# Moving the background matmuls of a fused attention and feed-forward kernel by one step

## The chip, the core and the metric
The kernel runs on one core of a Trainium2 chip. The metric is device time in microseconds: the median of three runs of the kernel before is 1022.14 us (1021.96 to 1023.54). The profiled execution is one of them and took 1021.96 us; its span, from the first to the last instruction, is 1020.1 us.

## The reference
One transformer layer with the norm after each part, in float32. There are 2 batches of 1024 rows of 512 columns.

```python
Q = (x @ Wq.T + bq)            # 32 query heads of 16
K = (x @ Wk.T + bk); V = (x @ Wv.T + bv)   # 8 key/value heads of 16
Q, K = _rope(Q, K)
scores = einsum('bhqd,bhkd->bhqk', Q, repeat(K, 4)) / sqrt(16)
w = softmax(scores)
attn = einsum('bhqk,bhkd->bhqd', w, repeat(V, 4))
x = layernorm(x + attn @ Wo.T + bo)
hdn = silu((x @ gate_w.T) * gate_s) * ((x @ up_w.T) * up_s)   # 1408 wide
x = layernorm(x + (hdn @ down_w.T) * down_s)
```

## The kernel before, in words
The five engines run programs of their own (`tensor`, `scalar`, `vector`, `gpsimd`, `sync` in the code, PE, ACT, DVE, POOL and SP in the profile), in order, and wait for each other through semaphores. A number in float32 is often held as a rounded high part and a low part, so that a product takes three fast matmuls (high by high, high by low, low by high).

Attention runs in 256 steps, numbered u, written (n, v) with u = 16n + v. There are 16 groups n (batch by key/value head). Eight steps are one pass over the 1024 keys for 512 queries, so "step 3 of 8" below means u % 8 == 3. In each step PE does, for g in 0 to 3, one score matmul of head g (`scores`, L478), which goes into one of three score banks in turn, and half of a maximum step (`advance`, `maxima_half`, L456), which computes scores that are only needed for their row maxima, some twelve steps ahead. Once per step it does `weigh` (L497), the product of the previous step's exponentials with V: after g = 3 in an even step, after g = 2 in an odd one. ACT takes the exponentials (L797); DVE takes the maxima, per step one whole reduction over two banks (L1008, 128x1024) and one in two halves (L1004, 128x512 each), the halves so that PE can refill a bank sooner. Two pairs of banks take the maximum steps in turn. The row maxima of sixteen maximum steps are complete at the end of each step 3 of 8: DVE joins them (L1024), POOL splits them in two parts (L1326), DVE transposes them (L1041), and in step 4 of 8 SP writes them to DRAM (`write_max`, L1572), waits until that has landed, and reads them back beside Q (L1575). The scores of the pass that begins four steps later wait for this (`max_in`, L471), since the maxima are subtracted inside the score matmul.

Eleven larger pieces of matmul work lie between the steps: six projections of Q or K for later heads (`project_at`, 24 matmuls each, L400), one product for V of batch 1 (`values_at`, 32 matmuls of 128x128, L437) and four parts of the output projection of batch 0 (`out_at`, 24 matmuls each, L523). `background(u)` issues one on PE. It needs two of the three score banks: `free_banks(u)` takes the bank just written by a score, and the one after it in turn. ACT (`evacuate_raw`, L783) or DVE (`add_values` L987, `add_rows` L1077) empties them. `norm_at` puts a layer norm of the rows of the piece before on DVE (`first_norm`, L1053 to L1061), which waits once for POOL. After a projection SP swaps halves by DMA (`swap_halves`), POOL rotates (`rope`), and ACT and POOL split the result (`rope_end`).

SP issues nearly all DMAs, on one queue and in program order: `gather` (L1557, L1563) brings K and Q of group n + 2 in twelve DMAs, `recip_at` sends reciprocals of the softmax sums out (L1602) and back broadcast (L1608), `finish` writes a pass's result (L1585). The eleven weight blocks of the feed-forward part are loaded (768 KB each, L1519, `A<-in_wf`) at the steps in `ffn_at`; at the steps in `low_at` POOL adds up their low bits (`add_low`, L1405 and L1407), which gives the flag by which the feed-forward part takes its path. That part follows from about 733 us on and is bound by PE.

Of the kernel before, what the change touches and what calls it, by code (L numbers as in the profile page):

```python
# [70 lines left out]
def post_ln_layer(nc, xT_d, x_d, wqk_d, wv_d, bqk_d, bv_d, wo_d, bo_d, wf_d, gs_d, us_d, ds_d,  # L71
# [6 lines left out]
    with ExitStack() as ctx:  # L78
# [121 lines left out]
        def bank(i):  # L200
            return PS2[:, i, :] if i < 3 else PV[:, :]
# [57 lines left out]
        stream = [(n, qt, g) for n in range(NG) for qh in range(2) for qt in range(4 * qh, 4 * qh + 4)  # L259
                  for g in (2, 0, 3, 1)]  # L260
        jobs = [(0, 1), (0, 2), (0, 3), (1, 4), (1, 0), (1, 1), (1, 2), (1, 3)]
        project_at = {(1, 10): 2, (4, 10): 3, (5, 2): 4, (6, 2): 5, (8, 2): 6, (8, 10): 7}
        rope_end = {(0, 1): (0, "h0"), (0, 2): (0, "h1"), (0, 3): (0, "out"),
                    (0, 4): (1, "rope"), (0, 8): (1, "h0"), (0, 10): (1, "h1"), (0, 11): (1, "out")}
        for at_u, j in project_at.items():
            u0 = 16 * at_u[0] + at_u[1] + 8
            rope_end.update({divmod(u0, 16): (j, "h0"), divmod(u0 + 2, 16): (j, "h1"), divmod(u0 + 3, 16): (j, "out")})
        values_at = (2, 10)
        out_at = {(10, 2): 0, (10, 10): 1, (11, 2): 2, (11, 10): 3}
        norm_at = {(10, 10): 0, (11, 2): 1, (11, 10): 2}  # L270
        recip_at = {(2, 13): 0, (4, 13): 1, (6, 5): 2, (8, 5): 3, (10, 5): 4, (12, 5): 5, (14, 5): 6}
        divide_at = {divmod(16 * n + v + 6, 16): kc for (n, v), kc in recip_at.items()}
        gather_at = {(n, {0: 13}.get(n, 5)): n + 2 for n in range(NG - 2)}
        x_at = {(part // 2, 8 * (part % 2)): (0, part) for part in range(4)}
        x_at.update({(2 + part // 2, 5 + 8 * (part % 2)): (1, part) for part in range(4)})
        ffn_at, low_at = {}, {}
        for i in range(FI):
            ffn_at.setdefault(divmod((181, 184, 189, 192, 204, 205, 207, 209, 221, 223, 228)[i], 16), []).append(i)
            low_at.setdefault(divmod(180 + 8 * (1, 1, 2, 3, 4, 4, 5, 5, 6, 6, 7)[i], 16), []).append(i)
        before_flag = 508  # L280

        crosswise = (0, 2, 1, 3)
# [37 lines left out]
        score_bank = {}  # L320
# [13 lines left out]
            return c if p == len(pieces(c)) - 1 else (c, p)  # L334

        def free_banks(u):
            last = score_bank[4 * u + 1, 0]
            return (last + 1) % 3, last

        def ffn_slots(x):  # L340
# [34 lines left out]
        def tensor(e):  # L375
# [335 lines left out]
            for u in range(SPLIT):  # L711
                at_u = divmod(u, 16)
                for g in range(4):
                    scores(u, g)
                    advance(1)
                    if len(pieces(4 * u + g)) == 2:
                        scores(u, g, 1)
                    if g == 1:
                        background(u)
                    if u >= 1 and g == (3, 2)[u % 2]:  # L720
                        weigh(u - 1)
                if at_u == (15, 1):
                    flag_sum()
                if at_u == (15, 2):
                    w.wait_ge(*dve_flag.at("flag"))
# [12 lines left out]
        def scalar(e):  # L738
# [190 lines left out]
            for u in range(SPLIT):  # L929
                at_u = divmod(u, 16)  # L930
                for g in range(4):
                    exponent(u, g)
                    if g == 1 and at_u in project_at:
                        for h, i in enumerate(free_banks(u)):
                            evacuate_raw(project_at[at_u], h, i)
                if u >= 1:
                    finish(u - 1)
                if at_u in rope_end and rope_end[at_u][1] in ("h0", "h1"):
                    round_half(rope_end[at_u][0], int(rope_end[at_u][1] == "h1"))
                if at_u == (15, 2):  # L940
                    w.wait_ge(*dve_flag.at("flag"))
# [11 lines left out]
        def vector(e):  # L953
# [318 lines left out]
            for u in range(SPLIT):  # L1272
                at_u = divmod(u, 16)
                maximum(next(steps))
                k = next(steps)
                if at_u in norm_at:
                    first_norm(False, 0, norm_at[at_u])
                if at_u == values_at:
                    for h, i in enumerate(free_banks(u)):
                        add_values(1, h, i)  # L1280
                if at_u in out_at:
                    add_rows(False, 0, out_at[at_u], [bank(i) for i in free_banks(u)])
                maximum(k)
                if at_u in recip_at:
                    reciprocal(recip_at[at_u])
                if at_u == (15, 0):
                    w.wait_ge(*pool_low.at((FI - 1, 2)))
                    e.tensor_reduce(lowb[:, :], lowsum, AX.X, ALU.max).then_inc(*dve_flag.next("max"))
                if at_u == (15, 1):
                    w.wait_ge(*pe_flag.at())  # L1290
                    e.tensor_scalar(flag[0:1, 0:1], slot_pair(before_flag % 2)[0:1, 0, 0:1], 0.0, None,
                                    ALU.is_gt).then_inc(*dve_flag.next("flag"))
                if at_u == (15, 2):
                    w.wait_ge(*dve_flag.at("flag"))
# [11 lines left out]
        def gpsimd(e):  # L1306
# [161 lines left out]
            for u in range(SPLIT):  # L1468
# [2 lines left out]
                    spread_of(2, (False, 0, norm_at[at_u]))  # L1471
                if u % 8 == 3 and apart(steps_done(u) // 16 - 1):
                    split_max(steps_done(u) // 16 - 1)
                if u >= 1 and divmod(u - 1, 16) in project_at:
                    rope(project_at[divmod(u - 1, 16)])
                if at_u in divide_at:
                    divide(divide_at[at_u])
                if at_u in rope_end:
# [367 lines left out]
```

## Time and profile before

| what | value |
|---|---|
| median of three runs | 1022.14 us |
| profiled execution | 1021.96 us |
| its span | 1020.1 us |
| PE busy | 1006.1 us (99%) |
| DVE busy | 797.0 us (78%) |
| ACT busy | 665.5 us (65%) |
| POOL busy | 274.2 us (27%) |
| chain that ended last | PE 93%, DVE 2% |
| mean granted clock of PE | 0.997 |

Busy time of PE counts overlapping matmuls and modelled ends, so 99% does not say that PE had no time to spare. What limits a stage is read from the gaps of the other engines in that stage, below.

### The profile page before, as it was taken

How to read it: one execution, taken by the hardware profiler on the slowest of the kernel's cores; microseconds unless marked ns; L12 is line 12 of the kernel's file. 1: busy time of each engine (PE TensorE's matmuls, PEld its weight loads, DVE VectorE, ACT ScalarE, POOL GpSimd, SP SyncE). 2: the span in 40 equal slices, each digit the busy share in tenths (PEclk: the TensorE clock that was granted, in tenths of full speed). 3: DMA queues.
4: the chain of work that ended last, by engine and by line, in shares of the span. 5: the costliest groups of instructions: out<-in, count | busy, mean ns of one | idle time of the engine just before them, and what ended most of it. 6: DMA issues, size and time to landing. Idle time of an engine off the chain costs nothing.

```text
span 1020.1 us, 15669 instructions
## 1 busy us (share of the span) xinstructions
PE 1006.1 (99%) x5852; PEld 532.3 (52%) x5852; DVE 797.0 (78%) x1131; ACT 665.5 (65%) x1345; POOL 274.2 (27%) x284
## 2 busy tenths in 40 slices
PE   8999999999999999999999999999999999999996
PEld 4643435334444333443444433333358888888885
DVE  6999797999787999779899999999713666562635
ACT  5179796888787988779767688888862430222221
POOL 4461030251245541246301063456000001000002
PEclk9999999999999999999999999999999999999998
DMA  6175316233224522444150447422438112221011
GB/s 245 50 208 137 94 55 203 59 97 92 55 81 116 101 81 42 83 104 111 35 81 13 121 140 167 105 100 63 150 109 221 63 42 58 67 65 19 0 42 44
DMA packets 64289, 94.81 MB, mean 93 GB/s; under 512 B 37520, under 2 KB 37776, under 8 KB 62128
## 3 DMA queue, kind: packets, MB, share of 16 engines
q1 hardware_dynamic: 63776, 93.10, 34.3%
q8 instruction: 48, 0.79, 0.3%
q10 hardware_dynamic: 432, 0.66, 0.2%
q14 instruction: 33, 0.27, 0.1%
HBM read 53.88 MB, written 27.00 MB: 79 GB/s over the span
## 4 chain that ended last, share of the span: by engine, by line
PE 93%; DVE 2%; issue 2%; POOL 1%; DMA 1%; ACT 0%; SPq 0%; POOLq 0%; DVEq 0%
PE PS L478 29%; PE PV L497 25%; PE PSA L567 16%; PE PS L584 6%; PE PSA L456 5%; PE PS L400 4%; PE PS L523 2%; PE PSA L523 2%; PE PV L584 2%; PE PS L437 1%; DMA A<-in_cosT 1%; DVE A L965 0%; ACT Bn L797 0%; PE PV L437 0%; PE PS L567 0%
## 5 line engine op out<-in xcount | busy, mean ns | idle before, releaser
L797 ACT ACTIVATE Bn<-PS 128x512 f32<-128x512 f32 x1128 | 536.2, 558 | 87.6 <-PE PS L478 74.5
L456 PE MATMUL PSA<-Kt,Qt 48*128 48x512 f32 x1010 | 382.9, 459 | 0.5 <-DVE nmx L1008 0.4
L478 PE MATMUL PS<-Qt,Kt 50*128 50x512 f32 x1128 | 382.0, 434 | 1.3 <-ACT Bn L797 1.1
L478 PEld LDWEIGHTS PS<-Qt,Kt 50*128 50x128 f32 x1128 | 183.3, 184 | 304.4 <-ACT Bn L797 279.0
L1004 DVE TENSOR_REDUCE nmx<-PSA 128x1 f32<-128x512 f32 x488 | 310.7, 677 | 30.8 <-PE PSA L456 30.8
L1008 DVE TENSOR_REDUCE nmx<-PSA 128x1 f32<-128x1024 f32 x261 | 317.4, 1218 | 19.5 <-PE PSA L456 16.5
L497 PE MATMUL PV<-Bn 128*32 128x512 f32 x2048 | 272.8, 605 | 0.0
L456 PEld LDWEIGHTS PSA<-Kt,Qt 48*128 48x128 f32 x1010 | 173.0, 183 | 8.6 <-issue 2.2
L567 PE MATMUL PSA<-x1Th,wr 128*128 128x512 f32 x344 | 135.3, 393 | 0.0
L567 PE MATMUL PSA<-x1Tl,wr 128*128 128x512 f32 x344 | 134.3, 390 | 0.0
L833 ACT ACTIVATE sg<-PSA,gs 128x512 f32<-128x512 f32 x43 | 29.7, 690 | 128.1 <-PE PSA L567 128.1
L1109 DVE SCALAR_TENSOR_TENSOR sg<-PSA,us,sg 128x512 f32<-128x512 f32 x43 | 32.2, 749 | 91.5 <-ACT sg L833 91.5
L1326 POOL CAST msp<-nmx 128x16 fp32r<-128x16 f32 x30 | 5.9, 198 | 285.0 <-DVE nmx L1024 285.0
L497 PEld LDWEIGHTS PV<-Bn 128*32 128x32 f32 x2048 | 40.3, 108 | 76.0 <-issue 65.0
L567 PEld LDWEIGHTS PSA<-x1Th,wr 128*128 128x128 f32 x344 | 64.6, 188 | 17.9 <-issue 3.6
L567 PEld LDWEIGHTS PSA<-x1Tl,wr 128*128 128x128 f32 x344 | 64.6, 188 | 13.4
L1412 POOL TENSOR_SCALAR ve<-mv 128x2 f32<-128x2 f32 (+1 forms) x11 | 2.9, 260 | 252.7 <-DVE mv L1056 252.7
L1129 DVE TENSOR_TENSOR hTl<-sg,hTh 128x512 fp32r<-128x512 f32 x38 | 27.9, 734 | 33.1 <-ACT hTh L846 33.0
L846 ACT CAST hTh<-sg 128x512 fp32r<-128x512 f32 x38 | 23.6, 621 | 43.9 <-DVE sg L1109 36.8
L584 PE MATMUL PS<-wr,hTh 128*128 128x512 f32 x114 | 44.6, 391 | 0.0
L584 PE MATMUL PS<-wr,hTl 128*128 128x512 f32 x114 | 44.5, 390 | 0.0
L1407 POOL TENSOR_TENSOR lowsum<-lowsum,lowf 128x512 f32<-128x512 f32 x32 | 41.0, 1282 | 2.6
(174 smaller groups left out, 896.0 us busy)
## 6 DMA issues: line engine op xcount, KB each, us to landing
Qt<-pscr SPq DMA_DIRECT2D x90, 128.0 KB, 5.2
A<-in_wf SPq DMA_DIRECT2D x11, 768.0 KB, 5.5
wr<-A SPq DMA_DIRECT2D x33, 256.0 KB, 2.8
pscr<-A SPq DMA_DIRECT2D x16, 512.0 KB, 3.5
vscr<-Bn SPq DMA_DIRECT2D x32, 256.0 KB, 2.7
Kt<-pscr SPq DMA_DIRECT2D x90, 64.0 KB, 2.7
A<-A SPq DMA_DIRECT2D x16, 256.0 KB, 3.7
Bn<-vscr SPq DMA_DIRECT2D x8, 512.0 KB
```

Of the source, the lines that this page charges most:

```text
L400: op = e.matmul(ps, v, t, start=first and i == 0, stop=last and end)
L456: op = e.matmul(slot_pair(s)[:, h, :], Qt[n % 3][p:p + NC_, g % 2, 128 * qt:128 * qt + 128], Kt[n % 3][p:p + NC_, 512 * h:512 * h + 512], ...
L478: e.matmul(score_tile(i)[:, cols], Kt[n % 3][rows, 128 * kt:128 * kt + 128], Qt[n % 3][rows, g % 2, 512 * qh + cols.start:512 * qh + cols. ...
L497: op = e.matmul(PV[32 * g:32 * g + 32, :], Bn[:, o:o + 32], Pb[c % NP_], start=(kt == 0), stop=(kt == 7), tile_position=(0, 32 * g))
L523: op = e.matmul(ps, t_, v, start=(k == 0 and i == 0), stop=(k == KT - 1 and i == len(pairs) - 1))
L567: op = e.matmul(gate_bank(x, q, j), v, t, start=(k == 0 and m == 0), stop=(k == KT - 1 and m == (1 if x else 0)))
L584: op = e.matmul(bank(t), v, t_, start=(i == 0 and m == 0), stop=(i == FI - 1 and end))
L797: e.activation(Pb[c % NP_][:, cols], score_tile(score_bank[c, p])[:, cols], ACT.Exp, scale=0.25).then_inc(*act_exp.next(piece(c, p)))
L1004: e.tensor_reduce(col, slot_pair(s)[:, h, :], AX.X, ALU.max, negate=True).then_inc(*dve_max[s].next((k, 0) if h == 0 else k))
L1008: e.tensor_reduce(nmx[:, hh % 2, c0:c0 + 1], slot_pair(s), AX.XY, ALU.max, negate=True).then_inc(*dve_max[s].next(k))
L1109: e.scalar_tensor_tensor(out=out, in0=gate_bank(x, q, 1), scalar=us[:, i:i + 1], in1=sg[q % 2], op0=ALU.mult, op1=ALU.mult).then_inc(*dve_ ...
L1407: e.tensor_tensor(lowsum, lowsum, lowf, ALU.add).then_inc(*pool_low.next((i, j)))
```

## The change
The eleven background pieces move from steps 2 of 8 to steps 3 of 8, and inside the step from behind g = 1 to behind g = 2 (all eleven steps are now odd), directly ahead of `weigh`. `free_banks` and ACT's evacuation follow. On DVE, in the steps of the values and of the output projection, the split maximum is taken apart: its first half stands ahead of the norm and the additions, its second half behind them. The second parts of `rope` stay in the steps where they were, `divide` comes two steps earlier, and the tables of weight loads and of POOL's sums are replaced by a formula.

```diff
-        project_at = {(1, 10): 2, (4, 10): 3, (5, 2): 4, (6, 2): 5, (8, 2): 6, (8, 10): 7}
+        project_at = {(1, 11): 2, (4, 11): 3, (5, 3): 4, (6, 3): 5, (8, 3): 6, (8, 11): 7}
-            u0 = 16 * at_u[0] + at_u[1] + 8
+            u0 = 16 * at_u[0] + at_u[1] + 7
-        values_at = (2, 10)
-        out_at = {(10, 2): 0, (10, 10): 1, (11, 2): 2, (11, 10): 3}
-        norm_at = {(10, 10): 0, (11, 2): 1, (11, 10): 2}
+        values_at = (2, 11)
+        out_at = {(10, 3): 0, (10, 11): 1, (11, 3): 2, (11, 11): 3}
+        norm_at = {(10, 11): 0, (11, 3): 1, (11, 11): 2}
-        divide_at = {divmod(16 * n + v + 6, 16): kc for (n, v), kc in recip_at.items()}
+        divide_at = {divmod(16 * n + v + 4, 16): kc for (n, v), kc in recip_at.items()}
-            ffn_at.setdefault(divmod((181, 184, 189, 192, 204, 205, 207, 209, 221, 223, 228)[i], 16), []).append(i)
-            low_at.setdefault(divmod(180 + 8 * (1, 1, 2, 3, 4, 4, 5, 5, 6, 6, 7)[i], 16), []).append(i)
+            ffn_at.setdefault(divmod(11 * 16 + 5 + 8 * (i // 2) + 3 * (i % 2), 16), []).append(i)
+            low_at.setdefault(divmod(11 * 16 + 4 + 8 * (1, 1, 2, 3, 3, 4, 4, 5, 5, 6, 7)[i], 16), []).append(i)
...
-            last = score_bank[4 * u + 1, 0]
+            last = score_bank[4 * u + 2, 0]
...
-                    if g == 1:
+                    if u >= 1 and g == (3, 2)[u % 2]:
                         background(u)
-                    if u >= 1 and g == (3, 2)[u % 2]:
                         weigh(u - 1)
...
-                    if g == 1 and at_u in project_at:
+                    if g == 2 and at_u in project_at:
...
-                if at_u in norm_at:
-                    first_norm(False, 0, norm_at[at_u])
-                if at_u == values_at:
...
-                maximum(k)
+                if at_u in norm_at or at_u in out_at or at_u == values_at:
+                    maximum(k, (0,))
+                    if at_u in norm_at:
+                        first_norm(False, 0, norm_at[at_u])
...
+                    maximum(k, (1,))
+                else:
+                    maximum(k)
...
-                if u >= 1 and divmod(u - 1, 16) in project_at:
-                    rope(project_at[divmod(u - 1, 16)])
+                if at_u in project_at:
+                    rope(project_at[at_u])
```

The loads stood at steps 181, 184, 189, 192, 204, 205, 207, 209, 221, 223 and 228; they stand at 181, 184, 189, 192, 197, 200, 205, 208, 213, 216 and 221 now.

On PE, around the product for V (L437), step (2, 10) of the kernel before. L478 is a score, L456 a maximum half, L497 `weigh`:

```order
L478 MATMUL PS<-Qt_109,Kt_110 128x512
L456 MATMUL PSA<-Kt_106,Qt_105 128x512
L437 MATMUL PS<-A 128x128 x32
L478 MATMUL PS<-Qt_109,Kt_110 128x512
L456 MATMUL PSA<-Kt_106,Qt_105 128x512
L478 MATMUL PS<-Qt_109,Kt_110 128x512
L456 MATMUL PSA<-Kt_106,Qt_105 128x512
L497 MATMUL PV<-Bn 32x512 x4
```

The same place in the changed kernel, step (2, 11):

```order
L478 MATMUL PS<-Qt_109,Kt_110 128x512
L456 MATMUL PSA<-Kt_106,Qt_105 128x512
L437 MATMUL PS<-A 128x128 x32
L497 MATMUL PV<-Bn 32x512 x4
L478 MATMUL PS<-Qt_109,Kt_110 128x128
L456 MATMUL PSA<-Kt_106,Qt_105 128x512
```

Two maximum halves stood between the piece and `weigh`; now `weigh` follows directly, and the maximum half behind it is the second of a split one.

On DVE, around the norm and additions of step (10, 10) of the kernel before. L1008 is a whole maximum, L1004 a half, L1053 to L1061 the norm, L1077 the additions, L1024 the join:

```order
L1008 TENSOR_REDUCE nmx<-PSA 128x1
L1053 BN_STATS st<-x1a 128x6 x2
L1056 BN_AGGR mv<-st 128x2 x2
L1061 TENSOR_SCALAR x1a<-x1a,mv,ve 128x512 x2
L1077 TENSOR_TENSOR x1a<-x1a,PS 128x512 x2
L1004 TENSOR_REDUCE nmx<-PSA 128x1 x2
L1008 TENSOR_REDUCE nmx<-PSA 128x1
L1004 TENSOR_REDUCE nmx<-PSA 128x1 x2
L1024 TENSOR_TENSOR nmx<-nmx 128x8
```

The same in the changed kernel, step (10, 11), where every line number is one lower:

```order
L1007 TENSOR_REDUCE nmx<-PSA 128x1
L1003 TENSOR_REDUCE nmx<-PSA 128x1
L1052 BN_STATS st<-x1a 128x6 x2
L1055 BN_AGGR mv<-st 128x2 x2
L1060 TENSOR_SCALAR x1a<-x1a,mv,ve 128x512 x2
L1076 TENSOR_TENSOR x1a<-x1a,PS 128x512 x2
L1003 TENSOR_REDUCE nmx<-PSA 128x1
L1023 TENSOR_TENSOR nmx<-nmx 128x8
```

The vector work lies between the two halves of one maximum, and the join comes directly after the second half.

On SP, steps 197 to 209 of the kernel before. `Kt` and `Qt<-pscr` are a gather, `vscr` a pass's result, `mscr` the maxima on their way out and in, `in_wf` the weight blocks:

```order
L1563 DMA Qt_109<-pscr 16x2048 x6
L1585 DMA vscr<-Bn 128x512
L1572 DMA mscr<-mrow 4x32x32
L1575 DMA Qt_107<-mscr 2x2x512 x2
L1519 DMA A<-in_wf 128x1536 x3
L1585 DMA vscr<-Bn 128x512
L1519 DMA A<-in_wf 128x1536
```

The same in the changed kernel:

```order
L1566 DMA Qt_109<-pscr 16x2048 x6
L1522 DMA A<-in_wf 128x1536
L1588 DMA vscr<-Bn 128x512
L1522 DMA A<-in_wf 128x1536
L1575 DMA mscr<-mrow 4x32x32
L1578 DMA Qt_107<-mscr 2x2x512 x2
L1522 DMA A<-in_wf 128x1536
L1588 DMA vscr<-Bn 128x512
L1522 DMA A<-in_wf 128x1536
```

Two weight blocks that stood behind the maxima's way out and in now stand ahead of it.

## Rows read from the trace of the kernel before

**Rows 1.** DVE's timeline, steps without a piece; start, duration, line, count, [idle before <-releaser].

```profile
301.00 1.22 DVE L1008 TENSOR_REDUCE nmx<-PSA 128x1 f32<-128x1024 f32 x1 [0.16 <-PE PSA L456]
...
305.94 1.23 DVE L1008 TENSOR_REDUCE nmx<-PSA 128x1 f32<-128x1024 f32 x1 [0.17 <-PE PSA L456]
...
307.08 1.28 DVE L1004 TENSOR_REDUCE nmx<-PSA 128x1 f32<-128x512 f32 x2
...
308.55 1.22 DVE L1008 TENSOR_REDUCE nmx<-PSA 128x1 f32<-128x1024 f32 x1
```

**Rows 2.** DVE's timeline around the projection of step (1, 10).

```profile
119.29 1.23 DVE L1008 TENSOR_REDUCE nmx<-PSA 128x1 f32<-128x1024 f32 x1 [0.16 <-PE PSA L456]
...
127.88 1.29 DVE L1004 TENSOR_REDUCE nmx<-PSA 128x1 f32<-128x512 f32 x2 [5.02 <-PE PSA L456]
129.77 1.22 DVE L1008 TENSOR_REDUCE nmx<-PSA 128x1 f32<-128x1024 f32 x1 [0.60 <-PE PSA L456]
...
132.38 1.22 DVE L1008 TENSOR_REDUCE nmx<-PSA 128x1 f32<-128x1024 f32 x1
```

**Rows 3.** PE's timeline around the same projection.

```profile
121.52 0.50 PE L400 MATMUL PS<-xh,wh 128*128 128x512 f32 x1
...
127.31 0.50 PE L478 MATMUL PS<-Qt,Kt 50*128 50x512 f32 x1
...
127.97 1.07 PE L497 MATMUL PV<-Bn 128*32 128x512 f32 x8
128.97 0.50 PE L478 MATMUL PS<-Qt,Kt 50*128 50x512 f32 x1
```

**Rows 4.** DVE's timeline, output projection with norm, step (10, 10).

```profile
521.26 1.22 DVE L1008 TENSOR_REDUCE nmx<-PSA 128x1 f32<-128x1024 f32 x1
...
534.31 1.22 DVE L1008 TENSOR_REDUCE nmx<-PSA 128x1 f32<-128x1024 f32 x1
```

**Rows 5.** Timeline of DVE and PE around the product for V, step (2, 10).

```profile
164.33 1.23 DVE L1008 TENSOR_REDUCE nmx<-PSA 128x1 f32<-128x1024 f32 x1 [0.17 <-PE PSA L456]
...
166.66 7.38 PE L437 MATMUL PS<-A 128*128 128x128 f32 x64
...
179.03 1.22 DVE L1008 TENSOR_REDUCE nmx<-PSA 128x1 f32<-128x1024 f32 x1
```

**Rows 6.** Timeline of ACT, exponentials ahead of step (1, 10) and in an undisturbed step 3.

```profile
120.98 0.49 ACT L797 ACTIVATE Bn<-PS 128x384 f32<-128x384 f32 x1
...
305.67 0.60 ACT L797 ACTIVATE Bn<-PS 128x512 f32<-128x512 f32 x1
```

**Rows 7.** Timeline of POOL and DVE around the projection of step (6, 2).

```profile
322.48 1.27 POOL L1352 TENSOR_TENSOR wl<-A,wh 128x512 fp32r<-128x512 f32 x1
...
330.10 1.29 DVE L1004 TENSOR_REDUCE nmx<-PSA 128x1 f32<-128x512 f32 x2 [5.77 <-PE PSA L456]
```

**Rows 8.** SP's timeline, from the end of a gather in step 197 on.

```profile
617.68 0.42 SPq L1585 DMA_DIRECT2D vscr<-Bn  x1
625.63 0.56 SPq L1572 DMA_DIRECT2D mscr<-mrow  x1
630.25 0.54 SPq L1575 DMA_DIRECT2D Qt<-mscr  x2
...
645.33 0.56 SPq L1572 DMA_DIRECT2D mscr<-mrow  x1
647.30 0.55 SPq L1575 DMA_DIRECT2D Qt<-mscr  x2
```

**Rows 9.** Busy time by stretch; the last two columns are DMA share and GB/s.

```profile
612.00:624.00 12.00, 12.00 (x83) 4.47 (x79) 11.76 (x15) 10.88 (x25) 0.24 (x1) 1.00 0.87 134
...
632.00:640.00 8.00, 8.00 (x56) 3.02 (x52) 7.85 (x11) 7.68 (x18) 1.24 (x1) 1.00 0.99 393
```

**Rows 10.** Timeline of PE and DVE where step 208 begins.

```profile
632.99 0.40 PE L456 MATMUL PSA<-Kt,Qt 48*128 48x512 f32 x1
...
633.86 1.22 DVE L1008 TENSOR_REDUCE nmx<-PSA 128x1 f32<-128x1024 f32 x1
```

More of the change, by code:

```diff
@@ L1275, in vector @@
                 k = next(steps)
-                if at_u in norm_at:
-                    first_norm(False, 0, norm_at[at_u])
-                if at_u == values_at:
[L1279 to L1282, printed above, removed]
-                maximum(k)
+                if at_u in norm_at or at_u in out_at or at_u == values_at:
+                    maximum(k, (0,))
+                    if at_u in norm_at:
+                        first_norm(False, 0, norm_at[at_u])
+                    if at_u == values_at:
+                        for h, i in enumerate(free_banks(u)):
+                            add_values(1, h, i)
+                    if at_u in out_at:
+                        add_rows(False, 0, out_at[at_u], [bank(i) for i in free_banks(u)])
+                    maximum(k, (1,))
+                else:
+                    maximum(k)
                 if at_u in recip_at:
```

## The prediction
> **What bounds the kernel now.** I read the page's engine shares first (they are in the table above): PE is busy 99% of the span, DVE 78%. Since that share counts modelled and overlapping matmuls, it does not tell who sets the pace of attention, so I took DVE's timeline in steps without a background piece [rows 1]. From the whole maximum at 301.00 to the same one two steps later, at 305.94, it is 4.94 us, and the only gap is 0.17 us. DVE's maxima set the pace, at 2.47 us a step; PE and ACT have slack there. So time is lost where DVE stands idle, and the reader is to look at DVE's gaps rather than at PE's work.
>
> Such gaps stand at each of the eleven background pieces. At step (1, 10) DVE waits 5.02 us for PE and then, once more, 0.60 us [rows 2]: PE is on the projection from 121.52 to 127.31, 5.79 us, issues two maximum halves and then does `weigh` from 127.97 to 128.97, 1.00 us [rows 3]. To price a piece I measure from the whole maximum of step 1 of 8 to the first one behind the join, in step 4 of 8. Without a piece that is 308.55 - 301.00 = 7.55 us [rows 1]. With the projection it is 132.38 - 119.29 = 13.09 [rows 2], with an output part 534.31 - 521.26 = 13.05 [rows 4], with the product for V 179.03 - 164.33 = 14.70 [rows 5]. A piece costs 5.54, 5.50 and 7.15 us now.
>
> **The change, part 1: the new place of the pieces.** The PE work is the same, so only the waits differ. I build the changed stretch by putting the projection into the quiet step of rows 1.
> - Start. A piece needs the bank behind the last score's, which in an odd step is that of g = 0, so it waits for that exponential. It runs from 305.67 for 0.60, to 306.27 [rows 6]. The piece starts 0.05 later, as it does before (120.98 + 0.49 = 121.47 [rows 6], start 121.52 [rows 3]): 306.32.
> - It takes 5.79: 312.11. `weigh` follows at once and takes 1.00: 313.11. Only then comes the maximum half. From PE's start of a score and half to DVE's start it is 127.88 - 127.31 = 0.57 [rows 2, 3]: DVE starts at 313.68.
> - The half takes 0.64 (half of the 1.28 for two [rows 1]): 314.32. From there to the next whole maximum, over the join, it is 308.55 - 308.36 = 0.19 [rows 1]: 314.51.
> - Without the piece this maximum starts at 308.55. The piece costs 5.96 us, against 5.54: plus 0.42.
>
> The 0.60 gap behind the piece does go, since the next maximum half is ready when the first is done; but `weigh` now lies inside the first gap and lengthens it by its 1.00. DVE's supply at the piece's start is nearly the same: here to 307.08 + 0.64 = 307.72, 1.40 us; before it ended at 127.88 - 5.02 = 122.86, 1.34 us [rows 1 to 3].
>
> For six projections this is 6 x 0.42 = 2.5 us. For the four output parts the way is the same (the norm and the first addition lie inside PE's piece in both orders, the second addition under `weigh` now), the new cost 5.96 less at most 0.1 for a slightly shorter piece: 5.9 - 5.5 = 0.4 each, 1.6 us. For V the piece takes 7.38 instead of 5.79 [rows 5]: 5.96 + 1.59 - 7.15 = 0.4. Together 4.5 us. What is not in the rows is how ACT and PE refill the banks right behind the piece; I bound a piece's difference by -0.58 (the 1.00 of `weigh` wholly hidden) and +0.7, and take 0.42, which follows the rows.
>
> One piece was late for another reason. At (6, 2) POOL ends the split of the weights only at 322.48 + 1.27 = 323.75, and DVE's gap is 5.77 instead of 5.02 [rows 7]. The piece is now needed one step, 2.47 us, later, behind 323.75: minus 0.75.
>
> Part 1: 4.5 - 0.75 = plus 3.7 us, from -7 to +7 by the bounds (11 x -0.58 - 0.75 and 11 x 0.7 - 0.75).
>
> **Part 2: the weight loads.** Two blocks of 768 KB move from steps 204 and 205 to 197 and 200. SP comes to them at about 617.7, right behind a gather [rows 8]. There the DMA engines are full: share 0.87 at 134 GB/s from 612 to 624 [rows 9]. Even without them the maxima's write of step 204 lands late: from its issue to the read's it takes 630.25 - 625.63 = 4.62 us, against 647.30 - 645.33 = 1.97 in a calm place [rows 8]. So something was still queued in front of it until about 630. Now 1.57 MB more is. At 393 GB/s, the rate of such loads [rows 9], that is 4.0 us at most of the engines' time; three blocks shared that stretch with a copy, and engines that were idle towards the end take a little of it. I take 3.7: the write has landed at 630.25 + 3.7 = 633.95.
>
> The read of the maxima must have landed before the scores of step 208. Before, PE started them at 632.99 without a gap [rows 10], at most 2.74 us behind the read's issue. With a read that takes between 1.97, as the write did, and 2.74, step 208 begins at 635.9 to 636.7, 2.9 to 3.7 us late. DVE has no supply but the split maximum in hand, and its next one starts at 633.86 without a gap [rows 10], so the delay passes to it whole. I take 3.2 us. The bounds are 0 (small transfers find free engines, or the backlog in front of them was not the same engines') and 4.2.
>
> The Trainium skill, in "DMA: Bandwidth & Descriptors", section "Queues, rings and completion order", says that each DMA engine takes its descriptors in the order of its ring, and that the semaphore fills only when every engine involved is through. The 4.62 us of rows 8 agree. By this rule the write cannot pass the loads, and the full term of part 2 stands; if small transfers passed large ones, the sum would lack 3.2 us.
>
> The later blocks (205, 208, 213, 216, 221) lie ahead of writes with more room and replace loads that were there. The blocks on POOL's list move with them; POOL is busy 27% of the span (same table).
>
> **Part 3: what costs nothing.** `divide` two steps earlier runs while POOL is idle, ahead of the next split of maxima. `rope` stays in its step; its data come later, since the swap's DMA now starts about when the join is due, and ACT asks for the rotated half only seven steps, 7 x 2.47 = 17 us, later. The swap's DMA also comes closer ahead of the maxima's write of the next step. If it cost nothing there, the read would have its usual room: the write is issued about four steps, 9.9 us, less the 1.4 us from the join, before the scores that need it, and takes 1.97, the read up to 2.74; that leaves over 3 us as cover, and if that were gone each microsecond over it would be lost at six places.
>
> **Sum.** 1021.96 (the profiled execution) + 3.7 + 3.2 = 1028.9 us. The median before is 0.2 us above that execution, so it stands for either; I say 1028.7.
>
> **Rivals.**
> - Only part 1. The maxima's write gets through, or the read is quick: 1025.7. For it: the delay needs the same engines to be backlogged; against it: the 4.62 us.
> - Only part 2. The new place costs nothing, because the two gaps merely change places: 1021.96 + 3.2 - 0.75 = 1024.4.
> - Neither: 1021.2 to 1022.5. For it: DVE's idle time per piece is mostly PE's 5.8 us in either order.
> - Faster. The gap behind `weigh` (0.60) goes and nothing takes its place, because PE enters the piece at 306.02 rather than 306.32 and DVE's work under it reaches to the end of `weigh`. Eleven pieces at -0.58 and the 0.75: 1021.96 - 7.1 = 1014.9. It decides at the first maximum half behind the piece: this rival needs DVE to start it not later than 6.4 us after PE enters the piece, as before (121.52 to 127.88). That the half stands behind `weigh` in the order speaks against it.
> - Slower still. The swap's DMA ahead of each of six maxima writes takes away more than the 3 us of cover, so that the scores of the next pass wait about 1 us at each: 1028.7 + 6 = 1035. Against it: the sizes above.
>
> **How the numbers follow.** Both parts 0.45; only part 1 0.22; only part 2 0.06; neither 0.10; faster 0.10; slower still 0.07. A difference under 0.2%, 2 us, can't be told from none here. Slower than 1024.2 are the first case, most of the second and of the third, and the last: 0.75. Same: 0.10 and 0.05 of the second and third: 0.15. Faster: 0.10. The range of 8 in 10 goes from 1022.5 to 1031.5: it leaves out the faster case, the slowest one and a few in a hundred of "neither". The likeliest case's own range is 1026 to 1031.
>
> **What the profile after would show.** At each projection one DVE gap of about 5.9 to 6.0 us before a single half (L1003), and no 0.60 gap behind it; from the whole maximum of step 1 to the one behind the join 13.5 us instead of 13.09. The gap at (6, 3) is like the others. On SP, two weight loads directly behind the gather, the maxima's write of step 204 landing 8 us or more after its issue, and the scores of step 208 waiting some 3 us for a DMA. I am wrong on part 1 if that distance stays 13.1 or falls; on part 2 if PE has no gap where step 208 begins; and on part 3 if scores wait at other passes, or ACT waits for POOL in the splits behind a projection.

## The result and the profile after

The changed kernel takes 1032.09 us (median of 4 runs, 1030.91 to 1033.06), the kernel before 1022.84 in the same comparison: a ratio of 1.0094, with a 95% interval of 1.0083 to 1.0106. Predicted were 1028.7 us and a range of 1022.5 to 1031.5. The direction and both places were right; the sum was 3.4 us short. The profiled execution of the changed kernel took 1032.56 us, its span is 1030.7 (1020.1 before).

I place the difference by DVE's joins. The join (L1024 before, L1023 after) comes once in 8 steps, so its distances cut attention into equal pieces. Worked out from the starts of these rows on DVE's timeline, in us:

| interval that holds | before | after | difference |
|---|---|---|---|
| nothing, behind quiet steps | 19.70 to 19.83 | the same | 0 |
| projection (1, 10) / (1, 11) | 25.27 | 25.76 | +0.49 |
| product for V | 26.91 | 27.35 | +0.44 |
| projections 3, 4 | 25.21, 25.33 | 25.70, 25.83 | +0.49, +0.50 |
| projection (6, 2) / (6, 3) | 26.05 | 25.64 | -0.41 |
| projections 6, 7 | 25.17, 25.25 | 25.62, 25.74 | +0.45, +0.49 |
| output parts, four | 25.24, 25.33, 25.21, 25.19 | 25.71, 25.80, 25.76, 25.76 | +0.47, +0.47, +0.55, +0.57 |
| the start of step 208 | 19.70 | 25.29 | +5.6 |

The pieces' rows add up to +4.5. The quiet intervals right behind a piece are longer by 0.03 to 0.13, and all quiet intervals up to step 208 together by +0.7. From there to the end the two kernels run alike. So part 1 cost 5.2 us (forecast 3.7) and part 2 5.6 us (forecast 3.2).

DVE's timeline of the changed kernel around the projection of (1, 11) (start, duration, line, count, idle before and releaser) answers to [rows 2]:

```profile
119.08 1.23 DVE L1007 TENSOR_REDUCE nmx<-PSA 128x1 f32<-128x1024 f32 x1 [0.17 <-PE PSA L456]
...
131.75 0.69 DVE L1003 TENSOR_REDUCE nmx<-PSA 128x1 f32<-128x512 f32 x1 [5.89 <-PE PSA L456]
132.54 0.17 DVE L1023 TENSOR_TENSOR nmx<-nmx 128x8 f32<-128x8 f32 x1
132.62 1.22 DVE L1007 TENSOR_REDUCE nmx<-PSA 128x1 f32<-128x1024 f32 x1
```

There is one gap of 5.89 us ahead of a single half and none of 0.60 behind it. From whole maximum to whole maximum it is 132.62 - 119.08 = 13.54 us (forecast 13.5, before 13.09 [rows 2]). PE's timeline at the projection of (8, 3) shows the order inside the gap: the bank's wait, the piece, `weigh` (L497) and then the next maximum half. It answers to [rows 3]:

```profile
412.27 0.39 PE L478 MATMUL PS<-Qt,Kt 50*128 50x512 f32 x1
...
413.12 0.50 PE L400 MATMUL PS<-xh,wh 128*128 128x512 f32 x1 [0.22 <-ACT Bn L796]
...
418.79 1.07 PE L497 MATMUL PV<-Bn 128*32 128x512 f32 x8
419.79 0.32 PE L478 MATMUL PS<-Qt,Kt 50*128 50x128 f32 x1
```

SP's timeline of the changed kernel answers to [rows 8]. Two weight loads (L1522) are issued where there were none, and the maxima's write of step 204 (L1575) is followed by its read (L1578) 8.04 us later, not 4.62:

```profile
622.46 0.42 SPq L1522 DMA_DIRECT2D A<-in_wf  x1
622.93 0.43 SPq L1588 DMA_DIRECT2D vscr<-Bn  x1
623.40 0.43 SPq L1522 DMA_DIRECT2D A<-in_wf  x1
630.60 0.56 SPq L1575 DMA_DIRECT2D mscr<-mrow  x1
638.64 0.56 SPq L1578 DMA_DIRECT2D Qt<-mscr  x2
```

PE's timeline at the start of step 208 answers to [rows 10]:

```profile
637.77 0.39 PE L478 MATMUL PS<-Qt,Kt 50*128 50x384 f32 x1
640.71 0.46 PE L478 MATMUL PS<-Qt,Kt 50*128 50x512 f32 x1 [2.55 <-DMA Qt<-mscr]
...
641.86 0.79 PE L456 MATMUL PSA<-Kt,Qt 48*128 48x512 f32 x1
642.58 1.93 PE L497 MATMUL PV<-Bn 128*32 128x512 f32 x8
```

and DVE's timeline there:

```profile
641.48 1.22 DVE L1007 TENSOR_REDUCE nmx<-PSA 128x1 f32<-128x1024 f32 x1 [2.55 <-PE PSA L456]
642.62 1.28 DVE L1003 TENSOR_REDUCE nmx<-PSA 128x1 f32<-128x512 f32 x2
645.74 1.22 DVE L1007 TENSOR_REDUCE nmx<-PSA 128x1 f32<-128x1024 f32 x1 [1.84 <-PE PSA L456]
...
648.60 0.69 DVE L1003 TENSOR_REDUCE nmx<-PSA 128x1 f32<-128x512 f32 x1 [1.04 <-PE PSA L456]
```

The wait that was forecast is 2.55 us. But two more gaps follow, 1.84 and 1.04, that no DMA ends. A matmul takes 0.79 us where it took 0.50 [rows 3], `weigh` 1.93 instead of 1.07. The busy time by stretch (engines' busy time, then the granted clock, the DMA share and GB/s) shows what goes with them; it answers to [rows 9]:

```profile
612.00:624.00 12.00, 12.00 (x83) 4.60 (x75) 11.94 (x16) 10.90 (x25) 4.92 (x5) 1.00 0.57 97
630.00:636.00 6.00, 6.00 (x43) 2.17 (x37) 6.00 (x10) 5.01 (x11) 4.63 (x6) 1.00 0.98 262
636.00:640.00 4.00, 2.16 (x17) 0.65 (x15) 2.81 (x4) 2.29 (x5) 3.64 (x5) 1.00 0.18 66
...
642.00:648.00 6.00, 6.00 (x26) 1.49 (x26) 3.72 (x5) 3.44 (x7) 1.18 (x1) 0.50 0.47 140
648.00:650.00 2.00, 2.00 (x11) 1.03 (x11) 1.39 (x2) 1.60 (x4) 0.00 (x0) 0.93 0.64 258
```

Behind the wait the granted clock of TensorE is 0.50, its lower level of 1.2 GHz, for some 7 us. The sum of the three gaps, 5.43 us, is nearly the +5.6 of the table. The prediction had no term for the clock.

### The profile page after: what moved, and what is told of

The parts are those of the page before. It is cut to its first block, busy times and chain, and to the rows that moved or that the text cites. A ratio compares the mean times of both kernels' runs of the same rounds, so it can differ in the third digit from the quotient of the medians.

```text
span 1030.7 us, 15669 instructions
## 1 busy us (share of the span) xinstructions
PE 1012.3 (98%) x5852; PEld 531.0 (52%) x5852; DVE 798.3 (77%) x1131; ACT 665.6 (65%) x1345; POOL 274.4 (27%) x284
## 4 chain that ended last, share of the span: by engine, by line
PE 91%; DVE 3%; issue 2%; DMA 2%; POOL 1%; ACT 1%; SPq 0%; POOLq 0%; DVEq 0%
PE PS L478 29%; PE PV L497 24%; PE PSA L567 15%; PE PS L584 6%; PE PSA L456 5%; PE PS L400 4%; PE PS L523 2%; PE PSA L523 2%; PE PV L584 2%; ACT Bn L796 1%; DMA mscr<-mrow 1%; PE PS L437 1%; DMA A<-in_cosT 1%; DVE nmx L1007 1%; DVE nmx L1003 0%
## 5 line engine op out<-in xcount | busy, mean ns | idle before, releaser
L478 PE MATMUL PS<-Qt,Kt 50*128 50x512 f32 x1128 | 386.0, 436 | 4.0 <-DMA Qt<-mscr 2.5
L456 PE MATMUL PSA<-Kt,Qt 48*128 48x512 f32 x1010 | 386.2, 460 | 0.5 <-DVE nmx L1007 0.4
L478 PEld LDWEIGHTS PS<-Qt,Kt 50*128 50x128 f32 x1128 | 183.1, 185 | 312.2 <-ACT Bn L796 285.0
L497 PE MATMUL PV<-Bn 128*32 128x512 f32 x2048 | 274.5, 608 | 0.0
L456 PEld LDWEIGHTS PSA<-Kt,Qt 48*128 48x128 f32 x1010 | 174.4, 184 | 9.1 <-issue 2.2
L497 PEld LDWEIGHTS PV<-Bn 128*32 128x32 f32 x2048 | 40.4, 108 | 76.3 <-issue 65.6
L1394 POOL TENSOR_TENSOR Bn<-Bn 128x1024 f32<-128x1024 f32 x8 | 19.1, 2383 | 98.9 <-DMA Bn<-rscr 98.9
```

Of the source, the lines that this page charges most:

```text
L456: op = e.matmul(slot_pair(s)[:, h, :], Qt[n % 3][p:p + NC_, g % 2, 128 * qt:128 * qt + 128], Kt[n % 3][p:p + NC_, 512 * h:512 * h + 512], ...
L478: e.matmul(score_tile(i)[:, cols], Kt[n % 3][rows, 128 * kt:128 * kt + 128], Qt[n % 3][rows, g % 2, 512 * qh + cols.start:512 * qh + cols. ...
L497: op = e.matmul(PV[32 * g:32 * g + 32, :], Bn[:, o:o + 32], Pb[c % NP_], start=(kt == 0), stop=(kt == 7), tile_position=(0, 32 * g))
```

## The experiments

The theory: part 1 costs about 5 us because a piece and `weigh` now lie in one stretch of PE without a score between them; part 2 costs a wait of 2.5 us behind two weight loads and some 3 us of half clock that the wait sets off. The rivals are in the expectations. All ratios are to the kernel before in the same comparison.

**The two parts apart.** e1 is the changed kernel with the old tables for the loads and for POOL's sums, e2 the kernel before with the new ones. Of e1's edit, the line for the loads:

```diff
-            ffn_at.setdefault(divmod(11 * 16 + 5 + 8 * (i // 2) + 3 * (i % 2), 16), []).append(i)
+            ffn_at.setdefault(divmod((181, 184, 189, 192, 204, 205, 207, 209, 221, 223, 228)[i], 16), []).append(i)
```

> The changed kernel with the tables of weight loads and of POOL's sums of the kernel before; the pieces stay at steps 3 of 8. Theory (the moved pieces cost about 5 us by themselves; the two loads at steps 197 and 200 make the maxima's write of step 204 late by 3.4 us, PE then idles 2.5 us and its clock falls to half for some 7 us, 5.6 us in all): the wait at step 208 and the half clock are gone, the write lands about 4.6 us after its issue, the time is 5 to 6 us under the changed kernel's, some 5 us (0.5%) over the kernel before. Rival (the loss at step 208 comes from the new place of the pieces or from the earlier divide, which move the whole schedule of DMAs): the wait and the loss of 5.6 us stay, time as the changed kernel, 0.9% over before.

> The kernel before with the new tables of weight loads and of POOL's sums alone; the pieces stay at steps 2 of 8. Theory: the wait at step 208 appears with the half clock behind it, plus 5 to 6 us over the kernel before (0.5 to 0.6%); the join distances at the eleven pieces stay at 25.2 us. Rival (the loads matter only together with the moved pieces): no wait at step 208, time as before.

e1: 1027.16 us, ratio 1.0046 (1.0033 to 1.0059), the intervals with pieces as in the changed kernel, 19.75 us at step 208. e2: 1028.10 us, ratio 1.0059 (1.0046 to 1.0072), intervals with pieces as before, and at step 208 24.17 instead of 19.70. With before at 1022.32 there, the parts are 4.8 and 5.8 us by the medians. They add up to 10.6, as much as the spans of the two kernels differ (the medians differ by 9.3), and neither is nothing. In e2's trace part 2 is smaller, 24.17 - 19.70 = 4.5 us, because the clock is low for some 3 us there and not for 7, although its wait is longer (2.81). Another 1.2 us of e2's profiled execution stand ahead of the join at 88.51 (87.30 before), where the clock falls too; see the last section. On SP's timeline of e1 write and read stand 3.01 us apart, less than the 4.62 of the kernel before, which no run explains:

```profile
630.78 0.56 SPq L1575 DMA_DIRECT2D mscr<-mrow  x1
633.79 0.54 SPq L1578 DMA_DIRECT2D Qt<-mscr  x2
```

and on that of e2 8.21 us:

```profile
627.07 0.56 SPq L1572 DMA_DIRECT2D mscr<-mrow  x1
635.28 0.56 SPq L1575 DMA_DIRECT2D Qt<-mscr  x2
```

e2 shows the clock's fall without the moved pieces. In its stretches the clock (third column from the end) is 0.50 with DMA share 0.00:

```profile
636.00:638.00 2.00, 0.60 (x6) 0.54 (x6) 0.00 (x0) 0.09 (x1) 1.86 (x3) 1.00 0.58 122
638.00:640.00 2.00, 1.81 (x14) 0.38 (x10) 1.82 (x3) 1.97 (x4) 1.86 (x3) 0.75 0.67 280
640.00:642.00 2.00, 2.00 (x14) 0.83 (x6) 0.60 (x1) 0.91 (x2) 0.82 (x1) 0.50 0.00 0
```

**One load instead of two.** e4 is the changed kernel with block 5 back at step 205; block 6 goes from 205 to 207, behind the write and the read in either place.

> The changed kernel with one of the two loads, block 5, put back from step 200 to step 205; block 4 stays at 197. Theory (each 768 KB ahead of the maxima's write costs its share of 3.4 us, and PE's room at step 208 is under 1 us): the write lands about 6.3 us after its issue instead of 8.0, PE idles about 0.8 us at step 208, the clock stays up, and the time is 4 to 5 us under the changed kernel's (0.5% over before). Rival (the wait is there as soon as any load stands ahead): the write lands 8 us after its issue and the time is as the changed kernel's.

Write and read stand 6.03 us apart (633.84 to 639.87), PE's gap is 0.54 us, and the interval takes 20.38 us, 0.6 over the quiet one; the clock stays up there. The forecast for the write was 6.3. So the second 768 KB cost 2.0 us (8.04 - 6.03), the first 1.4 to 3.0 (against 4.62 before and 3.01 in e1), and nearly all of part 2 hangs on the second load, since only with it the wait gets long. The time, 1030.07 us (ratio 1.0063, 1.0047 to 1.0078), is 2.0 us under the changed kernel's and not the 4 to 5 that were expected. It scatters from 1027.3 to 1032.06. The profiled execution (1030.87, mean clock 0.996) has a fall of the clock at 63 to 68 us; the two fastest, 1027.3 and 1027.91, have mean clocks of 0.997 and 0.999. The interval, 4.9 us under the changed kernel's 25.29, says more than the median.

**The wait filled.** Into PE's wait at step 208 go 13 matmuls of 48 rows (e3), five fp32 ones of 128 rows (e7) or three such (e11). The expectations of e7 and e11 also name POOL's split of e6, below, but their kernels do not have it: the interval of (6, 3) is 25.64 in both, as in the changed kernel, and the 0.9 us that they count for it could not come. The edit of e11:

```diff
+                if at_u == (13, 0):
+                    clear(bank_free[score_bank[4 * u, 0]])
+                    for _ in range(3):
+                        e.matmul(score_tile(score_bank[4 * u, 0]), Vflat[:, 0:128], Vflat[:, 0:512], start=True, stop=True)
```

> The changed kernel with 13 matmuls of 48 rows by 512 columns more on PE where step 208 begins, into the score bank that the next score overwrites: 13 x 0.23 = 3.0 us of work whose result nobody reads. Theory (3.1 of the 5.6 us are the half clock, and the clock falls because PE idles 2.5 us): the granted clock stays at its upper level (2.4 GHz) around step 208, DVE's gaps of 1.84 and 1.04 us behind the first one vanish, the first one grows by 0.3 to 0.5 us, and the time is 2.5 to 3 us under the changed kernel's (0.65% over before). Rival (the clock falls for another reason, for instance the DMA traffic, or the gaps of 1.84 and 1.04 us are not the clock's): the time grows by up to 0.5 us, the later gaps stay.

> The changed kernel with five fp32 matmuls of 128 rows by 512 columns put into TensorE's wait at step 208 (into a bank that is free by then), and POOL's split for (6,3) ahead of the bias addition. The same place filled with 48-row score matmuls did not hold the clock. Theory: with the array fully used through the wait the granted clock stays at 1.00 behind it, and the interval there goes from 25.3 to about 22.5 us (the 2.5 us wait itself stays, the some 3 us at half clock go); with -0.9 at (6,3) the time is about 1028.5. Rival A: the clock falls to 0.50 behind the wait whatever TensorE does in it (its cause is elsewhere, in the bulk loads or in the stretch before), 25.3 us stays, 1031. Rival B: the five matmuls run at fp32's four passes and last longer than the wait: 26 us or more, 1032.

> The changed kernel with POOL's split ahead and three fp32 matmuls of 128 rows by 512 columns in TensorE's wait at step 208, where five (4.56 us) kept the granted clock at 1.00 but lasted longer than the wait. Three last 2.7 us, about the wait's own length. Theory: clock stays at 1.00, the wait itself is all that is left, the interval takes 22.3 to 22.8 us (24.3 with five, 25.3 with none), and the time is 2.5 to 3 us below the changed kernel's with another 0.9 off at (6,3): about 1028.5. Rival: three are too few to hold the clock, it falls as with none or with the 48-row ones, 25.3 us and 1031.

| filler at step 208 | lasts | DVE's gaps | interval | clock behind it |
|---|---|---|---|---|
| none | | 2.55, 1.84, 1.04 | 25.29 | 0.50 |
| 13 of 48 rows | 3.30 | 3.23, 1.65, 0.55 | 25.28 | 0.50 |
| 5 fp32 of 128 rows | 4.56 | 4.45 | 24.30 | 1.00 |
| 3 fp32 of 128 rows | 2.84 | 2.73 | 22.56 | 1.00 |

The time was 1031.7 with e3 (ratio 1.0078, 1.0065 to 1.0091), 1031.75 with e7 (ratio 1.0085, 1.007 to 1.0101) and 1030.6 with e11 (1.008, 1.0063 to 1.0096). Both e7 and e11 missed the 1028.5 of their expectations. The medians do not tell e11 from the changed kernel (their intervals overlap); the span does, 1027.7 against 1030.7, and so does the interval at step 208. PE in e11:

```profile
637.89 2.84 PE L716 MATMUL PS<-Bn 128*128 128x512 f32 x6
640.66 0.49 PE L478 MATMUL PS<-Qt,Kt 50*128 50x512 f32 x1
...
642.27 1.06 PE L497 MATMUL PV<-Bn 128*32 128x512 f32 x8
```

The scores start when they did without a filler, 640.66, yet `weigh` takes 1.06 us and not 1.93. With the wait left as it is and the clock held, 22.56 - 19.70 = 2.9 us are left: that is the term that the prediction sized 3.2. The other 25.29 - 22.56 = 2.7 us are the clock. My theory in e3 was wrong, though: a busy PE is not enough. Its 13 matmuls filled the wait without a gap (PE, then its stretches) and the clock fell all the same:

```profile
638.05 3.30 PE L717 MATMUL PS<-Qt,Kt 48*128 48x512 f32 x13
```

```profile
638.00:640.00 2.00, 2.00 (x12) 1.63 (x11) 1.04 (x2) 0.71 (x2) 1.87 (x2) 1.00 0.03 7
640.00:642.00 2.00, 2.00 (x11) 1.72 (x10) 0.00 (x0) 0.18 (x1) 1.90 (x2) 0.74 0.76 195
642.00:644.00 2.00, 2.00 (x10) 0.49 (x10) 1.72 (x2) 1.89 (x4) 1.27 (x1) 0.50 0.49 203
```

The fillers that held it differ from these in more than the rows: they are fp32 products with other operands, of 0.47 us a record and not 0.25. Which of this counts is not shown.

**Is it the wait or the loads?** In the kernel before, PE waits at the calm step (7, 0) for small memsets that POOL starts behind the last scores, 36 of them in e8, 74 in e12:

```diff
+                if at_u == (7, 0):
+                    w.wait_ge(*pool_idle.at())
```

> The kernel before with a wait of TensorE added at step (7,0), far from any bulk load: ahead of that step's scores it waits for 36 small memsets that POOL starts when the last scores of the step before are done (about 3.5 us, of which TensorE still has 1 us of weigh, so some 2.5 us idle). Theory (a wait of some 2.5 us among 48-row score matmuls is enough to lower the granted clock, wherever it is): the granted clock falls to 0.50 behind the wait, matmuls take 0.79 instead of 0.50 us, and that interval grows by 2.5 plus about 3 us, 19.7 to 25. Rival (the fall at step 208 needs the bulk loads that run there): the clock stays at 1.00 and the interval grows by 2.5 us or less, 22.

> The kernel before with TensorE's wait at step (7,0) made longer: 74 small memsets on POOL instead of 36, of which 36 left TensorE 1.37 us idle, the granted clock at 1.00 and the interval at 21.2 us (19.7 without). With 74 it should be idle for 2.6 to 2.7 us, as long as at step 208 in the changed kernel (2.55). Theory (the fall behind step 208 is what an idle of this length does wherever it is): the granted clock falls to 0.50 behind the wait and the interval takes 25 us, 5.3 over 19.7. Rival (the bulk loads of step 208 are needed for it): the clock stays at 1.00 and the interval takes 22.5.

e8's wait was only 1.37 us and not the 2.5 expected, the clock stayed at 1.00 and the interval took 21.22 us, 1.5 more: the wait and nothing else (1023.89 us, ratio 1.0014, 1.0003 to 1.0025). The clock and the interval are those of the profiled execution, 1022.88 us; four of the other seven took 1024.3 to 1026.36 at mean clocks of 0.994 to 0.996, so it was low for longer somewhere in them; where, no trace shows. e12's PE waited 2.62 us:

```profile
366.35 0.50 PE L480 MATMUL PS<-Qt,Kt 50*128 50x512 f32 x1 [2.62 <-POOL idleb L1492]
...
367.97 1.86 PE L499 MATMUL PV<-Bn 128*32 128x512 f32 x8
369.76 0.79 PE L480 MATMUL PS<-Qt,Kt 50*128 50x512 f32 x1
```

and its stretches, with hardly a DMA:

```profile
366.00:368.00 2.00, 1.44 (x12) 0.70 (x12) 0.83 (x1) 1.11 (x3) 0.30 (x10) 1.00 0.00 0
368.00:371.00 3.00, 3.00 (x16) 0.96 (x14) 1.59 (x3) 1.95 (x4) 0.00 (x0) 0.52 0.00 0
```

The interval took 24.05 us, 4.3 more than 19.7: 2.7 for the wait and 1.5 for a clock at 0.5 for some 3 us (1026.83 us, ratio 1.0048, 1.0032 to 1.0065). The loads are not needed for the fall; a wait of this length is enough. It was shorter here than at step 208, so the expected 5.3 was too much; what sets its length no run tells.

**What the place of a piece costs.** e5 puts `weigh` ahead of the piece in the changed kernel; e10 is the kernel before with its projections one tile later, behind the third tile of the even step; e9 cuts the projections into halves, two steps apart.

```diff
-                        background(u)
                         weigh(u - 1)
+                        background(u)
```

> The changed kernel with one thing else: at the moved place the weigh product of the step before is issued ahead of the inserted piece, not behind it. In the changed kernel the piece waits 0.21 us for ACT to free its bank and starts then, weigh comes behind it, and DVE's gap ends with the scores behind weigh. Theory: what the new place costs over the old (about 0.5 us a piece) is PE time between two scores: piece 5.8, weigh 1.0 and the wait for a bank all lie in one stretch in which DVE has only what is left in the ring of banks. The order of the two within the stretch takes only the bank wait away: 0.2 us for each of 11 pieces, about -2 us (1030), intervals with a projection 25.5 instead of 25.75. Rival A: the order does not matter at all, 1032 and 25.75. Rival B: the piece was cheaper before because weigh was ahead of it by then with DVE still having a whole tile to reduce; then the intervals go back to 25.25 and the time to 1027. The wait for step 208 stays in all three (25.3 us there).

> The kernel before with its six projections one tile later in the same step: behind the scores of the third tile, not of the second; that is in an even step, five tiles behind a weigh and one tile ahead of the next. The values, output parts and loads stay. Theory (TensorE's work between two scores counts as one stretch only where weigh stands next to the piece; a tile of scores between them is enough for DVE to reduce something): intervals with a projection stay at 25.25 within 0.15 us, time 1022.3 within 1. Rival (every tile nearer to weigh costs, since the banks are not full again by then): 25.5 to 25.8 as in the changed kernel, time 1024 to 1025.5. Rival on the other side (the place before had a second, short gap of 0.60 us behind the piece, which a later place loses): 24.7 and 1019.

> The kernel before (its loads, its values and output parts) with the six projections cut in two: half 0 two steps ahead of half 1, each between the scores of the third tile and weigh, in the bank freed longest ago, and POOL's split ahead of the bias addition. Theory (what a piece costs is its length on PE less what DVE still has to reduce from the banks when it starts): each half is 2.9 us and uses that store once, so an interval with a projection costs 4.6 to 5.1 us over a quiet one instead of 5.5, -0.4 to -0.9 for each of six and -0.75 for the split, total -3 to -6 us, about 1018.5. Rival: the store of 3 banks is not filled again within two steps (DVE and PE run at nearly the same rate), so the second half costs its whole 2.9 us and the first 2.9 less the store: same as before apart from the split, 1021.6. Rival on the other side: with one half only the next scores wait for ACT to empty the bank, which two halves in a row hide; 0.5 us for each of 12, 1027.

| projection | DVE's gaps | interval | next interval |
|---|---|---|---|
| before, behind the 2nd tile | 5.02, 0.60 | 25.27 | 19.75 |
| e10, behind the 3rd, even step | 4.86, 0.96 | 25.49 | 19.77 |
| after, behind the 3rd, odd step, ahead of `weigh` | 5.89 | 25.76 | 19.86 |
| e5, the same, behind `weigh` | 5.61 | 25.46 | 20.28 |
| e9, two halves | 3.16, 3.07 | 26.30 | 19.85 |

(At the projection of step (1, 10) or its neighbour.) e10: 1023.19 us, ratio 1.0002 (0.9992 to 1.0012). Five of its projections cost 0.22 to 0.30 us more in the trace and that of (6, 2) 0.18 less; 1.1 us in all are too little for that median. The expectation of no difference held for the time and not for the interval. So about half of part 1's price comes with the tile nearer to `weigh`, without any wait of PE. The rest is near the 0.22 us that PE waits for its bank; that this wait is the rest was not tried alone. e5 took this wait away and got another: with the piece directly ahead of the next score, that score waits for ACT to empty the piece's bank,

```profile
264.26 0.49 PE L478 MATMUL PS<-Qt,Kt 50*128 50x512 f32 x1 [0.30 <-ACT A L782]
```

and the next interval pays 0.4 us more: 1034.02 us, ratio 1.0112 (1.0096 to 1.0127), slower than the changed kernel by 1.9 by the medians, whose intervals overlap, and by 1.0 by the spans (1031.7 and 1030.7). The interval of 25.5 that the theory gave for e5 came; none of its three times did. e9 came near the time of its last rival, 1028.35 us, ratio 1.006 (1.0046 to 1.0074), but not by its mechanism: no score behind a half waits for ACT. PE waits for its bank ahead of each half instead, 0.29 and 0.21 us. Each half makes a gap of its own on DVE, here around step (8, 3):

```profile
415.01 0.69 DVE L1008 TENSOR_REDUCE nmx<-PSA 128x1 f32<-128x512 f32 x1 [3.14 <-PE PSA L462]
...
423.20 0.69 DVE L1008 TENSOR_REDUCE nmx<-PSA 128x1 f32<-128x512 f32 x1 [3.06 <-PE PSA L462]
```

A half and `weigh` are 2.9 + 1.0 = 3.9 us of PE, of which some 0.8 are covered, as much as for a whole piece (5.8 + 1.0 - 5.9 = 0.9). What DVE holds is used once per stretch, but `weigh` enters both stretches and eats what the second use brings. This sum gives 6.2 us of gaps against 5.9, and the interval grew by 0.54, so a part stays open. So what counts is the length of PE's stretches without a maximum half, not PE's work alone.

**POOL's late split.** e6 is the kernel before with POOL's split of the weights ahead of its bias addition at (5, 12), and no longer behind it:

```diff
                 if at_u == (5, 12):
+                    split_w(1, u)
                     add_bo(0, u)
```

> The kernel before with one thing else: at step (5,12) POOL splits the weights for the projection of (6,2) ahead of the bias addition instead of behind it. Theory: the longer gap of DVE there (5.77 against 5.02 us, rows of the kernel before) is this late split, so the gap goes to 5.0 and that interval from 26.05 to 25.3; total -0.75 us (1021.6 where before is 1022.3). Rival: the split is not what came last (a semaphore between, or the addition being late hurts another), the gap stays 5.77 and the time the same.

It did what was expected; the gap of 5.77 us in [rows 7] is down to 4.89,

```profile
329.11 1.29 DVE L1004 TENSOR_REDUCE nmx<-PSA 128x1 f32<-128x512 f32 x2 [4.89 <-PE PSA L456]
```

and the interval takes 25.17 us instead of 26.05. The time is 1021.58 us against 1022.61, ratio 0.9992 (0.9983 to 1.0001): the lowest median of all the kernels here, though its interval does not quite exclude no change. The 0.88 us in the trace are the better evidence.

## Why the prediction was right in kind and wrong in size

- **What bounds the kernel.** Right. The time that was lost stands in gaps of DVE. "PE has slack there" was too simple: PE's stretch without a maximum half sets the gap.
- **Part 1, the mechanism.** Right: one gap of 5.89 us (forecast 5.9 to 6.0), no second one, 13.54 us (13.5). Mis-sized was the term per piece: 0.42 and 0.4 were forecast, 0.44 to 0.57 came in the pieces' own intervals (4.9 us for ten, where 4.1 were forecast) and 0.7 in the quiet intervals, most of it right behind the pieces, where the prediction said it could not see how the banks are refilled. The late split was worth 0.88 us (e6) and not 0.75, which goes the other way. Together, 0.8 + 0.7 - 0.1, that is about the 1.5 us by which part 1 was short.
- **Part 2, the write and the wait.** Right: 8.04 us from write to read (forecast some 8.3), a wait of 2.55 us at step 208, worth 2.9 in the interval of e11 (3.2). The rule of the Trainium skill ("DMA: Bandwidth & Descriptors", section "Queues, rings and completion order"), that each DMA engine takes its descriptors in ring order, agrees with the traces: from write to read 3.01 us with neither load moved (e1), 6.03 with one (e4), 8.04 with both.
- **Part 2, the step that failed.** "The delay passes to it whole. I take 3.2 us", with an upper bound of 4.2. The delay passed whole and did not end there: TensorE's granted clock fell to 0.50 behind the wait, 2.7 us more (25.29 against 22.56 in e11). The bounds held only what a DMA can delay; the clock's fall was a term at nothing, without a reason. Neither miss alone would have left the range: 1028.7 + 2.7 = 1031.4 and 1028.7 + 1.5 = 1030.2 lie below 1031.5. It took both.
- **Part 3.** Right in that no score waits at another pass and divide, rope and swap cost nothing that the intervals show.
- **The rivals.** "Only part 1" fell with e2, "only part 2" and "neither" with e1, "faster" with the gap of 5.89. The sum with the clock's 2.7 and part 1 at 5.2 would have been 1021.96 + 5.2 + 2.9 + 2.7 = 1032.8, against the profiled 1032.56; that adds up measured terms, and shows only that no large one is missing.

## What to carry to other kernels

Price a piece of background work by the stretch that it makes on the producer between two deliveries to the engine that sets the pace, everything that is glued to it included; a gap that vanishes behind it may only have moved inside. When a change adds a wait to TensorE, look what kind of work stood there: behind waits of 2.55 to 2.95 us among matmuls on 48 rows the clock fell each time and cost 1.5 to 2.7 us, half as much to as much again as the wait, and such a term belongs in the range, also for a shorter wait, since the clock fell behind some of 1.1 to 1.35 us as well (next section). And a small transfer on which the next pass waits should not be issued behind bulk loads of the same queue: count the bytes ahead of it.

## What the runs showed of the hardware that I had not expected

- The granted clock fell to 0.50 behind waits of 2.55 (after), 2.62 (e12), 2.81 (e2) and 2.95 us (e5, at step 208), and not behind 1.37 (e8) nor at the pieces, where DVE is idle for 5.9 us but TensorE works on. It stayed low for 3 to 7 us and cost 1.5 to 2.7.
- These lengths are no threshold. At about 62 us every one of the 14 traces has a wait of TensorE for ACT, of 1.08 to 1.35 us. In four of them (e7 1.08, e2 1.10, e4 1.21, e10 1.35) the clock fell behind it, in the other ten (1.12 to 1.35) it did not. TensorE in e7 and, with the longest wait and no fall, in e12:

```profile
62.21 0.79 PE L478 MATMUL PS<-Qt,Kt 50*128 50x512 f32 x1 [1.08 <-ACT Bn L800]
...
62.93 1.93 PE L497 MATMUL PV<-Bn 128*32 128x512 f32 x8
```

```profile
62.56 0.50 PE L480 MATMUL PS<-Qt,Kt 50*128 50x512 f32 x1 [1.35 <-ACT Bn L801]
```

- Back-to-back matmuls on 48 rows in place of the wait did not hold the clock (e3), fp32 matmuls on 128 rows did (e7, e11), in the one traced execution of each. Whether it is the rows or something else of these instructions was not tried apart.
- The falls at 62 to 69 us cost 1 to 3 us by the first join behind them. The times of the kernel before lie in two groups, 1021.7 to 1022.6 at mean clocks of 0.997 to 0.999 and 1023.3 to 1024.9 at 0.994 to 0.997, probably for the same reason; only the lower group has a trace. For effects under 2 us the interval between two joins in a trace told more than the medians.
